# Banded attention: projections in quarters between the value products, and two semaphores for the rows of maxima

## The reference

```python
x = x + _L0_attn_a_ref(_layernorm(x, axis=-1), ...)     # x: 8 x 1024 x 256, 16 heads of 16

qkv = x @ Wqkv + bqkv
q, k, v = jnp.split(qkv, 3, axis=-1)
...
scores = jnp.stack([jnp.einsum('bhnd,bhnd->bhn', q, _shift(k, delta, n)) for delta in OFFSETS], axis=-1) * scale
scores = scores + pos_bias.T[None, :, None, :]
...
alpha = jax.nn.softmax(scores, axis=-1)
for i, delta in enumerate(OFFSETS):
    out = out + alpha[..., i:i + 1] * _shift(v, delta, n)
...
gate = jax.nn.sigmoid(x @ Wgate + bgate)
return flat * gate @ Wout + bout
```

## Time and profile before

| | |
|---|---|
| median of three executions | 3741.56 us |
| profiled execution, time | 3749.66 us |
| its span in the profile | 3747.8 us |
| mean granted TensorE clock | 0.896 |
| banded attention, batches 0 to 7 | 182.57 to about 1562 us |
| PE busy, of the span | 2978.7 us (79%) |
| DVE, ACT, POOL busy | 1708.6, 1422.1, 749.2 us |

### The profile page before, as it was taken

The page is one execution under the profiler, slowest core; times in us unless marked ns, Lnnn a source line. Parts: engine busy times, 40 slices in busy tenths (PEclk is TensorE's granted clock), DMA queues, the critical chain, the costliest instruction groups (busy, mean ns, idle before and its releaser), DMA issues. The chain is left out here.

```text
span 3747.8 us, 100386 instructions
## 1 busy us (share of the span) xinstructions
PE 2978.7 (79%) x45340; PEld 1702.7 (45%) x45340; DVE 1708.6 (46%) x2811; ACT 1422.1 (38%) x1390; POOL 749.2 (20%) x523
## 2 busy tenths in 40 slices
PE   0487777777777777589956999999989999997898
PEld 0255545455555555434443444444444444443345
DVE  5133334343434333360165566666665666564302
ACT  0244344343444443241002555454455454453310
POOL 0333232333333232000002112121112121110000
PEclk9688879898888889689957999999999999998996
DMA  5323222233223232128713222222222232202394
GB/s 132 86 64 90 66 78 72 73 81 78 75 78 81 64 87 58 25 92 341 292 12 85 60 55 59 52 52 52 60 52 53 55 66 55 57 19 93 131 421 171
DMA packets 233159, 344.17 MB, mean 92 GB/s; under 512 B 113306, under 2 KB 141796, under 8 KB 216356
## 3 DMA queue, kind: packets, MB, share of 16 engines
q1 hardware_dynamic: 207508, 310.01, 28.5%
q10 hardware_dynamic: 25232, 27.83, 3.1%
HBM read 266.15 MB, written 69.24 MB: 89 GB/s over the span
## 5 line engine op out<-in xcount | busy, mean ns | idle before, releaser
L1382 DVE TENSOR_REDUCE b_tops<-b_slot 128x8 f32<-128x1024 f32 x576 | 680.4, 1220 | 359.1 <-PE b_slot L1239 180.1
L1419 ACT ACTIVATE b_probs<-b_slot 128x1024 f32<-128x1024 f32 x576 | 583.1, 1023 | 552.3 <-PE b_slot L1239 396.5
L1259 PE MATMUL b_outT_ps<-b_probs,b_v 128*17 128x128 f32 (+3 forms) x4608 | 319.8, 385 | 6.2 <-ACT b_probs L1419 5.6
L1239 PE MATMUL b_slot<-b_q_stack,b_k_stack 99*128 99x512 bf16 (+3 forms) x1280 | 276.1, 323 | 43.3 <-DVE b_tops L1382 32.8
L481 POOL COPY a_q_far<-a_q_near 96x1024 bf16<-96x1024 bf16 x128 | 257.4, 2040 | 253.1 <-PE a_slot L560 188.1
L1186 POOL TENSOR_SCALAR_AFFINE_SELECT b_probs<-b_probs 128x1024 f32<-128x1024 f32 x128 | 139.8, 1093 | 809.0 <-ACT b_probs L1419 809.0
L849 ACT ACTIVATE a_k_far<-a_k_near 96x1024 bf16<-96x1024 bf16 x128 | 257.8, 2064 | 86.8 <-DMA a_k_near<-parts_near_dram 70.3
L1239 PE MATMUL b_slot<-b_k_stack,b_q_stack 96*128 96x512 bf16 (+3 forms) x1280 | 266.4, 323 | 29.6 <-DVE b_tops L1382 20.9
L761 DVE TENSOR_REDUCE a_tops<-a_slot 128x16 f32<-128x1024 f32 x128 | 156.3, 1222 | 260.9 <-PE a_slot L560 259.9
L813 ACT ACTIVATE a_probs<-a_probs 128x1024 f32<-128x1024 f32 x128 | 133.4, 1053 | 325.6 <-DVE a_probs L752 296.1
L1239 PEld LDWEIGHTS b_slot<-b_q_stack,b_k_stack 99*128 99x128 bf16 x1280 | 107.0, 99 | 205.3 <-DVE b_tops L1382 61.9
(11 more groups left out here) (219 smaller groups left out, 4479.5 us busy)
## 6 DMA issues: line engine op xcount, KB each, us to landing
f_w_ring<-in_L_ffn_w_dram SPq DMA_DIRECT2D x128, 1024.0 KB, 9.3
parts_near_dram<-a_parts ACTq DMA_DIRECT2D x96, 256.0 KB
parts_dram<-b_parts SPq DMA_DIRECT2D x96, 256.0 KB
a_k_near<-parts_near_dram SPq DMA_DIRECT2D x128, 128.0 KB, 2.9
b_k_stack<-parts_dram SPq DMA_DIRECT2D x64, 256.0 KB, 6.8
a_q_near<-parts_near_dram SPq DMA_DIRECT2D x64, 192.0 KB, 2.9
b_q_stack<-parts_dram SPq DMA_DIRECT2D x32, 384.0 KB, 4.5
values_dram<-a_v_stage SPq DMA_DIRECT2D x16, 544.0 KB, 4.3
```

Of the source, the lines that this page charges most:

```text
L1239: ins = pe.matmul(dst[:, at:at + top - lo], own[0:rows, head, P * tile:P * tile + P], other[0:rows, head, lo:top], start=True, stop=True)
L1259: ins = pe.matmul(outT_ps[32 * h:32 * h + HD + 1, first:last], v1[b % 2][:, j, HG * g + h, :], src[:, base + first:base + last], start=u = ...
L1382: ins = dve.tensor_reduce(out, src, AX.X, ALU.max)
L1419: act.activation(probs_of(b, g, u, h)[:, :], slot_of(step)[:, :], ACT.Exp).then_inc(taken_act, 1)
```

## The change

Projections no longer stand whole. `quarter` does one fourth of a `q`, `k`, `v` or `op` (for `q` and `k` one product of 512 columns, for `v` and `op` three of 256, one of these the bias), and `weave` puts the fourths between the value products: behind P0, P2, P4 and P6 of the near steps, and behind each of the last four far ones. The `k` of group 3 is spread over all. Which step goes where, in batches with both neighbours:

| group | places before | places after |
|---|---|---|
| 0 | `ot`, `gmul`; `gate` 0; behind the products `at` 0, `gate` 1, `op` 0 | `ot`, `gmul`; `gate` 0; `at` 0; among the products `op` 0, `at` 1, `op` 1; behind them `gate` 1 |
| 1 | `at` 1, `op` 1, `ot`, `z`, `zt`; behind the products `q` 0 | `ot`, `z`, `zt`; among the products `q` 0, `v` 0; behind them `k` 0 |
| 2 | `k` 0, `ot`, `v` 0; behind the products `q` 1 | `ot`; among the products `q` 1, `v` 1 |
| 3 | `ot`, `v` 1; behind the products `k` 1 | `ot`; among the products `k` 1 |

The second part gives each pair of heads its own semaphore for the rows of maxima: the first `S` waits for four DMAs and the third for the other four. `mred_done` is folded into `mred_chain` to make room for the extra semaphore.

```diff
@@ band_schedule
+            return [("ot", b - 1, 3), ("gmul", b - 1)], [], [("gate", b, 0)], [("at", b - 1, 0)], [("at", b - 1, 1)], [("gate", b, 1)]
...
+        return {1: (("q", b + 1, 0), ("v", b + 1, 0), None), 2: (("q", b + 1, 1), ("v", b + 1, 1), None), 3: (None, None, ("k", b + 1, 1))}[g]
+
+    def weave(steps, filler, after):
+
+        out = []
+        for n, step in enumerate(steps):
+            out.append(step)
+            if filler and n in after:
+                k = after.index(n)
+                out.append(("piece", filler, k) if k < 3 else filler)
+        return out
...
-            seq += ([("fparts",) + after] if more else []) + turned(n + 4) + near + place[4] + ([("fp",) + after, ("mred",) + after] if more else [])
-            seq += far[0:4] + ([("mt",) + after, ("mrow",) + after] if more else []) + operands(n + 5)
-            seq += far[4:8] + [("ote", b, g)] + place[5]
+            early, late, through = between(b, g)
+            products = weave(near, early, (0, 2, 4, 6)) + place[4] + ([("fp",) + after, ("mred",) + after] if more else [])
+            products += far[0:4] + ([("mt",) + after, ("mrow",) + after] if more else []) + operands(n + 5)
+            products = weave(products + weave(far[4:8], late, (0, 1, 2, 3)), through, (1, 5, 11, 17))
+            seq += ([("fparts",) + after] if more else []) + turned(n + 4) + products + [("ote", b, g)] + place[5]
@@ band_attention
+        mrows_in = [sem(f"mrows_in{pair}") for pair in range(2)]
...
-        MROW = 16 * HG * 2
+        MROW = 16 * HG
...
-                        if h == 0:
-                            pe.wait_ge(mrows_in, MROW * count("mrow", "mrow", b, g))
+                        if h % 2 == 0:
+                            pe.wait_ge(mrows_in[h // 2], MROW * count("mrow", "mrow", b, g))
...
+                        for n in quarters:
+                            ins = quarter(dst, *whole, n)
+                        if kind != "piece":
+                            ins.then_inc(filled, 1)
```

More of the change, by code:

```diff
@@ L562, in products, with quarter @@
                     return ins
+                def quarter(dst, kind, b, part, n):
+                    if kind in ("q", "k"):
+                        kd, c = divmod(n, 2)
+                        return pe.matmul(dst[:, c * 512:(c + 1) * 512],
+                                         wqk[:, "qk".index(kind), kd, 8 * part:8 * part + 8, :].rearrange("p h d -> p (h d)"),
+                                         zT[:, kd, c * 512:(c + 1) * 512], start=kd == 0, stop=kd == KD - 1)
+                    weights, bias = {"v": (wv, V_BIAS), "gate": (wgate, GATE_BIAS), "op": (wout, OUT_BIAS)}[kind]
+                    to = dst[:, n * D:(n + 1) * D]
+                    for kd in range(KD):
+                        tokens = flatT[:, (n * KD + kd) * P:(n * KD + kd + 1) * P] if kind == "op" else \
+                            zT[:, kd, (4 * part + n) * P:(4 * part + n + 1) * P]
+                        pe.matmul(to, tokens, weights[:, kd, :], start=kd == 0, stop=False)
+                    return pe.matmul(to, ones_rows[:, :], bias_rows[:, bias, :], start=False, stop=True)
                 def stacks(b, g, pair):
@@ L643, in _ @@
                         ins.then_inc(filled, 1)
[L644 to L662, removed]
-                            ins = pe.matmul(dst[:, i * D:(i + 1) * D], ones_rows[:, :], bias_rows[:, bias, :], start=False, stop=True)
-                        ins.then_inc(filled, 1)
@@ new lines, in _ @@
+                    elif kind in ("piece", "q", "k", "v", "gate", "op"):
+                        whole, quarters = (step[1], (step[2],)) if kind == "piece" else (step, (3,) if ("piece", step, 0) in seq_pieces else range(4))
+                        dst = slot_of(whole)
+                        if 0 in quarters:
+                            if whole[0] == "op":
+                                pe.wait_ge(taken_act, count("taken_act", "at", *whole[1:]))
+                            else:
+                                pe.wait_ge(taken_act, count("taken_act", "zt", whole[1], 1))
+                            slot_free(whole)
+                        for n in quarters:
+                            ins = quarter(dst, *whole, n)
+                        if kind != "piece":
+                            ins.then_inc(filled, 1)
@@ L768, in _ @@
                             if prev := before(b, g):
-                                dve.wait_ge(mrows_in, MROW * count("mrow", "mrow", *prev))
+                                for rows in mrows_in:
+                                    dve.wait_ge(rows, MROW * count("mrow", "mrow", *prev))
                             ins = dve.tensor_copy(neg_rows[:, 1, :].rearrange("c (r a) -> c r a", r=LINKS),
```

53 lines of the change are left out of this document (24 added, 29 removed).

## The result

| | before | after |
|---|---|---|
| median | 3747.44 us (4 executions) | 3601.5 us (4 executions, 3594.65 to 3609.01) |
| profiled execution | 3749.66 us | 3609.01 us |
| its span, mean granted clock | 3747.8 us, 0.896 | 3607.2 us, 0.907 |

The ratio, both kernels on one chip, is 0.961, with a 95% interval of 0.9576 to 0.9644: 3.9% less. The forecast was 3612, the range 3545 to 3690. The profiled execution of after is the longest of its four, 7.5 above the median.

What follows compares the result with a forecast made beforehand. No engine full: a chain, PE closest at 74%, with instruction-fetch gaps. Per batch 152.2 + 9 = 161.2 against 179.2 us; six times 18.0 is 108, plus 6 and 16 makes 130; 3620 profiled, median 3612, range 3545 to 3690.

Steps and rivals of the forecast that it cites:

- The reading of "issue": Gaps ahead of value products are waits for the next 256 instructions, every 3.5 us; 21.7 us a batch falls near 5.
- The groups: Banded attention, four groups of a batch at full clock: 43.3, 39.9, 38.1 and 30.9 us, sum 152.2.
- The clock: Time lost at 1.2 GHz in a batch's matmuls: 9 us, as before, with bounds 0 and 31.
- The scores' stretches: First score to first value product, groups 0 to 3: 17.1, 17.8, 19.5 and 13.9 us.
- Group 2 behind the first value product: From first value product to the next group's first score: 7.3 + 4.4 + 6.9 = 18.6 us.
- the split wait does nothing: Rival: ACT's copy of the rows comes late behind part of `q`; 20 us less gain, 3632; chance within the forecast's 0.55.
- Group 3 behind the first value product: From first value product to the next first score: 11.0 to `mt`, 0.4 for a slot, 5.6 behind, together 17.0 us.
- Batches 0 and 7: Gains in the first and last batch of banded attention: 6 us and 16 us.
- The gaps did give way: Rival denied here: gaps ahead of value products stay beside the quarters, 3724 us, about no change; chance 0.12.
- The turns did not decide: Rival denied here: stretches before products stay at 20 us in groups 0, 2, 3; 3678 us; chance 0.14.
- The clock neither paid back nor stayed up: Two rivals: quarters at 1.2 GHz, 31 us a batch, 3766, chance 0.06; no clock loss, about 3550, chance 0.13.
- One sign: In the profile after, first scores wait for DMAs only in group 3 and in batch 7.

Runs made afterwards that it cites:

- with one move each: Changed kernel with either ACT's copy of the maxima ahead of a part of `q` (3584.94 us), or statistics ahead of `k` 0 in group 1 (3581.95 us).
- with both: Changed kernel with ACT's copy of the maxima ahead of a part of `q` and statistics ahead of `k` 0 in group 1, run twice: 3573.43 and 3563.66 us.
- the last experiment: `mx` 0 ahead of `zt` 0 in group 1, against the changed kernel that already had the copy and statistics moved: 3577.36 us, ratio 0.9562.

## Why the prediction was right, point by point

**The reading of "issue" was right.** At most one packet every 3.3 us, a gap behind 128 products, and P that follows the number of instructions are shown. The block of 256 instructions that the Trainium skill gives ("Runtime: NRT & Kernel Launch", Instruction fetch mechanics) is in the trace; its rule that fetching is hidden is not borne out: 21.7 us a batch before, and 3.4 us of P for 240 instructions left out. "Issue" fell to 4.3 where I had written near 5.

**The groups.** Forecast at a full clock 43.3, 39.9, 38.1 and 30.9, with 9 for the clock over all four; measured, clock included, 44.8, 42.3, 41.9 and 32.1. That the batch came out at 161.0 against 161.2 is luck in part, for the terms cancel: with its 5.5 us of clock taken off, as below, it is 155.5 against 152.2.

- *The clock* was sized too high. `gate` and the quarters, by form, in the six batches:

```profile
L589 PE MATMUL a_slot<-a_zT,a_wqk 128*128 128x512 f32 x192 | 114.0, 694 | 2.1 <-issue 2.1
L597 PE MATMUL a_slot<-a_wgate,a_zT 128*128 128x256 f32 x192 | 61.7, 450 | 1.4 <-DVE a_probs L771 1.4
L597 PE MATMUL a_slot<-a_wout,a_zb 128*128 128x256 f32 x192 | 54.7, 406 | 0.6 <-issue 0.6
L597 PE MATMUL a_slot<-a_wv,a_zT 128*128 128x256 f32 x192 | 54.3, 405 | 0.0
```

  `v` fell from 76.9 to 54.3, as low as `op` was before (54.1), so next to none of it is at 1.2 GHz now; it stands late in the products. `q` and `k` lose 114.0 - 24 x 3.70 = 25.2, `gate` some 7.5: 33 us, 5.5 a batch and not 9. The loss at the head of the products, in the first quarters of `q`, is new. Narrow products run slow there too, which neither sum counts: in batch 5's group 1 the first 32 take 1.06 us, where 32 take 0.59 at a full clock, and the next 64 take 1.86 instead of 1.09.
- *The scores' stretches* were sized too low in group 0: 19.6 against 17.1, the one step of that group that failed (P with C is 25.1 against 26.2). Some 1.2 of these 2.5 us are `gate` at 1.2 GHz, which the forecast held under the clock. Groups 1, 2 and 3 are 18.8, 19.8 and 13.8 against 17.8, 19.5 and 13.9.
- *Group 2 behind the first value product*: 22.1 against 18.6. 2 us of it are the rival "the split wait does nothing": ACT's copy did come late behind a part of `q`, as it said, and moving it gave 2.0 back. I had ruled that wait out for groups 0 to 2 because 6.9 us of work stand behind `mt`; where the copy is late, the way to the first score takes longer than that. The other 1.5 us can be found in the near products: in batch 5 they take 9.3 us with `q` and not 7.3. At 1.2 GHz the first 32 and part of the first quarter (1.59 instead of 1.12) lose 0.9, and each further quarter holds up the products by some 1.05 us and not 0.9. Group 1, 23.5 against 22.1, has the same head, with 2.2 us at 1.2 GHz in batch 5.
- *Group 3 behind the first value product*: 18.2 against 17.0. Here I had counted in packets, three and a bit to `mt`, and rightly: in batch 5 `mt` starts 11.7 us behind the first product, against 11.0.

**Batches 0 and 7.** Batch 0 gave 13.7 instead of 6, batch 7 13.9 instead of 16. But batch 0 took 148.2 us after, 153.5 and 152.8 with one move each, and 148.0 and 146.5 with both, so some 5 us of it are not tied to the edit. The profiled execution forecast at 3620 took 3609.0, and 8 of these 11 us are batch 0.

**The rivals.** The gaps did give way. The turns did not decide over the whole, since group 3 starts its products 13.8 us behind the first score; but groups 0 and 2 do so at 19.6 and 19.8, next to the rival's 20. They are next: 39.1 us of waits for them are the largest item in the waits after (29.1 and 10.0), and the last experiment ended on ACT's turn and the slot behind it. The clock neither paid back nor stayed up; it went from 0.86 to 0.88. One sign did not come: first scores were to wait for DMAs only in group 3 and in batch 7, and they do behind group 2's products as well, where C falls by 2.0 once ACT's copy comes first.

## What to carry over

Where TensorE runs long rows of narrow products with a weight load each, count instructions and not columns: at these rates 128 such products cost 3.5 us, not 1.9, and a quarter of a projection put in every 32 to 72 of them costs about half of its own time: P of group 2 grew by 3.5 us, from 15.1 to 18.6, for the whole of `q` (3.5) and three quarters of `v` (3.9). A projection is such a filler, but the cover that it gave elsewhere goes with it: look for what the moved work hid (here DMAs behind `mt`; one wait for all of them cost 34 us in the traces and 49 by the ratios), and let nothing of the fillers' follow-up work stand ahead of the step that everyone waits for on ACT and DVE.

## What the runs showed of the hardware

- Packets of 256 instructions never came closer than 3.2 us in this stage, in the five traces in which this was measured (3.25 before, 3.34 after, 3.27 and 3.30 with fewer products, 3.23 with whole projections). At the two places looked at closely a packet took 1.1 to 1.3 us to move, and started 1.1 to 1.2 us after the products had resumed. A stretch that comes behind wide matmuls behaves as if it had a packet in hand: after, 128 far products run at once in 1.57 us behind batch 5's near ones, where 128 in a bare stretch are followed by a gap of 1.6.
- With both semaphores of the rows on the first score, its wait for them is named "issue" (58.9 us) and hardly any longer "DMA" (5.7 instead of 30.6). So that name alone does not say fetching; the place and the instruction queue's packets do.
- Batch 0 of 146.5 to 153.5 us in kernels that differ little there: what makes the difference was not looked into.
